# Attention of a fused layer: probabilities turned by DMA and VectorE in place of TensorE

## The reference

```
kv_c = kv @ W_kvc                                     # 256 keys x 128
q_c  = q @ W_dq ; q_nope, q_rope = q_c @ W_uq, q_c @ W_qr     # 16 heads
scores = (q_nope . k_nope + rope(q_rope) . rope(k_rope)) * scale
good = (k_ids <= seg_id) & (k_ids >= seg_id - 8)
attn = softmax(where(good, scores, NEG))
out  = (attn @ v).reshape(b, lq, H * HD) @ W_o
x = x + out
```

## Time and profile before

| | |
|---|---|
| runs | 3063.78, 3070.87, 3072.26 us; median 3070.87 |
| profiled execution | 3065.81 us, its span 3064.0 us |
| PE busy | 3032.5 us, 99% |
| PE weight load / DVE / ACT / POOL busy | 86% / 73% / 45% / 40% |
| attention loop | about 1040 to 2355 us of the span |
| TensorE's clock | full, except 3.4 us at half speed about 1015 us and again about 2424 us |

### The profile page before, as it was taken

How to read it: one execution, slowest core, us unless ns; L and a number is a source line. 1 busy time by engine, 2 the same in 40 slices (tenths; PEclk the granted TensorE clock), 3 DMA queues, 4 the chain that set the end, 5 groups by cost and what they waited for, 6 DMA issues and landing times.

```text
span 3064.0 us, 50062 instructions
## 1 busy us (share of the span) xinstructions
PE 3032.5 (99%) x18181; PEld 2636.4 (86%) x18181; DVE 2248.4 (73%) x5504; ACT 1379.9 (45%) x3399; POOL 1224.1 (40%) x1190
## 2 busy tenths in 40 slices
PE   9999999999999999999999999999999999999999
PEld 6777777899899799999999999999998788888887
DVE  7989999755677788888888888888887533333342
ACT  4655555433566455555555555555555211111111
POOL 9999999454333433333222333333311111111120
PEclk9999999999999999999999999999999999999999
DMA  4444442298899511111111111111102211111110
GB/s 153 131 144 138 129 130 86 86 307 299 220 265 284 189 49 49 49 49 43 49 42 49 49 49 36 49 38 47 49 29 81 88 56 55 55 49 43 46 42 14
DMA packets 179011, 292.41 MB, mean 95 GB/s; under 512 B 22616, under 2 KB 73952, under 8 KB 178768
## 3 DMA queue, kind: packets, MB, share of 16 engines
q1 hardware_dynamic: 145200, 193.24, 20.4%
q0 software_dynamic: 23344, 77.35, 7.9%
q10 hardware_dynamic: 10224, 18.62, 1.6%
HBM read 177.38 MB, written 111.76 MB: 94 GB/s over the span
## 4 chain that ended last, share of the span: by engine, by line
PE 92%; DVE 3%; DMA 2%; POOL 1%; ACT 1%; issue 1%; SPq 0%; POOLq 0%; DVEq 0%
PE f_Y L559 4%; PE t_U L1818 4%; PE f_Y L560 4%; PE f_Y L562 4%; PE t_U L1819 4%; PE t_U L1820 4%; PE g_O L2640 4%; PE g_PH L2628 4%; PE g_PH L2627 4%; PE g_PH L2626 4%; PE g_O L2642 4%; PE g_O L2641 4%; PE t_T L1794 3%; PE f_Y L554 2%; PE t_PO L1804 2%; PE t_PO L1805 2%
## 5 line engine op out<-in xcount | busy, mean ns | idle before, releaser
L1954 ACT ACTIVATE t_pr<-t_sm,t_nb 128x256 f32<-128x256 f32 x512 | 256.7, 502 | 418.5 <-DVE t_nb L2176 418.5
L2372 POOL TENSOR_TENSOR t_r<-t_r 128x256 f32<-128x256 f32 x128 | 95.8, 749 | 696.7 <-DVE t_r L2155 387.5
L2696 DVE CAST g_hh<-g_hf 128x512 fp32r<-128x512 f32 x128 | 67.8, 530 | 382.0 <-PE g_O L2642 380.2
L2667 ACT ACTIVATE g_hf<-g_PH,b1g 128x512 f32<-128x512 f32 x128 | 88.1, 688 | 528.3 <-PE g_PH L2628 457.0
L1360 POOL TENSOR_TENSOR c_kf<-c_vt,c_ct 128x512 f32<-128x512 f32 x256 | 284.5, 1129 | 5.9 <-ACT c_vt L775 3.2
L2186 DVE TENSOR_SCALAR t_pr<-t_pr,t_rw 128x256 f32<-128x256 f32 x512 | 256.7, 501 | 18.1
L559 PE MATMUL f_Y<-c_kh,c_th 128*128 128x512 f32 x540 | 250.8, 465 | 0.0
L562 PE MATMUL f_Y<-c_kl,c_th 128*128 128x512 f32 x540 | 213.7, 396 | 0.7 <-DVE c_kl L1072 0.7
L560 PE MATMUL f_Y<-c_kh,c_tl 128*128 128x512 f32 x540 | 213.4, 395 | 0.0
L2640 PE MATMUL g_O<-g_w,g_hh 128*128 128x512 f32 x512 | 200.1, 391 | 5.0 <-DVE g_hl L2698 5.0
L1818 PE MATMUL t_U<-t_voh,t_oth 128*128 128x512 f32 x512 | 202.0, 394 | 0.0
(11 more groups left out here) (375 smaller groups left out, 9974.9 us busy)
## 6 DMA issues: line engine op xcount, KB each, us to landing
xs<-c_zero SPq DMA_DIRECT2D x71, 256.0 KB, 4.6
f_xg<-xs SPq DMA_DIRECT2D x284, 64.0 KB
ys<-f_yt ACTq DMA_DIRECT2D x71, 256.0 KB, 5.1
f_xg<-xn SPq DMA_DIRECT2D x40, 256.0 KB, 4.9
c_xt<-x SPq DMA_DIRECT2D x32, 256.0 KB, 3.5
c_cr<-ctx SPq DMA_DIRECT2D x32, 256.0 KB, 4.0
c_ct<-ctxh SPq DMA_DIRECT2D x32, 256.0 KB, 4.9
c_t<-kt SPq DMA_DIRECT2D x32, 256.0 KB, 5.0
```

## The change

- The probabilities are turned without TensorE. ScalarE now also does `normalise(N)` (t_pr from t_sm with the inverse sum as scale, written in the order of the store), VectorE only the reciprocals (`inverses`). SyncE stores t_pr to DRAM (fp, 256 KB, runs of 512 bytes) and, when the store has landed, loads it back as t_pq (256 KB, runs of 2 KB). VectorE turns the 32x32 blocks (t_ptq), ScalarE rounds (t_pth), GpSimd makes t_ptl.
- The queries of a head now stand in another order, so t_xo is loaded and stored in four DMAs of 32 partitions each, and the store of x3 moves from GpSimd's queue to SyncE; the store of x2 for later sequences moves from SyncE to GpSimd.
- The loop is one step deeper: av(N-3) and vo(N-5) where av(N-2) and vo(N-4) stood. t_T is free and serves as second t_PO.
- Order on each engine: turn, rounding and low part come first in the step (on VectorE behind the maxima), the rest behind. GpSimd's mix is cut in four parts over steps 11 to 14.
- At the end `dense_first(0, 0)`, the first block of the dense part, stands ahead of the last two vo. Six dummy matmuls (`keep_busy`) at N = 2 are gone. In dense group 0 the rows are stored and loaded two blocks earlier in SyncE's list.

```
     def pturn(N):                                   # VectorE
-        w.wait_ge(*A["pth", N])
-        ve.tensor_tensor(m.ptl[:, N % 2, :, :], m.T[:, :].rearrange("p (k c) -> p k c", k=2), f32(m.pth[:, N % 2, :, :]),
-                         ALU.subtract).then_inc(*V("ptl", N))
+        w.wait_ge(*Q[f"pl{N % 2}"]["pl", N])
+        w.wait_ge(*P["av", N - 2])
+        ve.transpose(m.ptq[:, N % 2, :, :].rearrange("p k q -> p (k q)").rearrange("p (k c t) -> p c k t", k=4, c=4),
+                     m.pq[:, N % 2, :].rearrange("p (c k f) -> p c k f", c=4, k=4)).then_inc(*V("pt", N))
...
+    def probabilities(N):                           # SyncE, in every step
+        w.wait_ge(*A["nm", 2 * N + 1])
+        w.wait_ge(*V["pt", N - 4])
+        sp.dma_start(d["fp"][N % 4].rearrange("(i p f) -> p i f", i=4, f=128),
+                     m.pr[:, N % 2, :, :, :, :].rearrange("p i k t f -> p i (k t f)")).then_inc(*Q[f"ps{N % 2}"]("ps", N))
+        w.wait_ge(*Q[f"ps{N % 2}"]["ps", N])
+        w.wait_ge(*V["pt", N - 2])
+        sp.dma_start(m.pq[:, N % 2, :], d["fp"][N % 4].rearrange("(p l) -> p l", p=128)).then_inc(*Q[f"pl{N % 2}"]("pl", N))
...
+    def normalise(N):                               # ScalarE
+        w.wait_ge(*Q[f"ps{N % 2}"]["ps", N - 2])
+        for t in range(2):
+            x, k4 = 2 * N + t, (2 * N + t) % 4
+            w.wait_ge(*V["rc", x])
+            ac.activation(m.pr[:, N % 2, :, :, t, :], m.sm[:, k4, :].rearrange("p (i k f) -> p i k f", i=4, k=2), ACT.Copy,
+                          scale=m.rw[:, k4, 1:2]).then_inc(*A("nm", x))
...
+    def pturn(N):                                   # GpSimd
+        w.wait_ge(*A["pth", N])
+        gp.tensor_tensor(m.ptl[:, N % 2, :, :], m.ptq[:, N % 2, :, :], f32(m.pth[:, N % 2, :, :]), ALU.subtract).then_inc(*G("ptl", N))
...
-    def pturn(N):                                   # TensorE
-        w.wait_ge(*V["nm", 2 * N + 1])
-        w.wait_ge(*V["vw", 4])
-        w.wait_ge(*V["ptl", N - 1])
-        for kb in range(2):
-            for t in range(2):
-                i = pe.transpose(m.T[:, 256 * kb + 128 * t:256 * kb + 128 * t + 128], m.pr[:, N % 2, t, 128 * kb:128 * kb + 128], ident)
-        i.then_inc(*P("pt", N))
...
-        if 1 <= N <= TOTAL:
-            pturn(N - 1)
-        if 2 <= N <= TOTAL + 1:
-            av(N - 2)
+        if 3 <= N <= TOTAL + 2:
+            av(N - 3)
-        if N == 2:
-            keep_busy(pe, m.PU[0], ident, 6)
+        if N == TOTAL + 2:
+            dense_first(pe, w, K, 0, 0)
...
-        if g + 1 < GROUPS and 6 <= k < 10:
-            dense_rows_out(sp, w, K, 4 * (g + 1) + k - 6)
-        if g + 1 < GROUPS and 7 <= k < 11:
-            dense_rows_in(sp, w, K, 4 * (g + 1) + k - 7)
+        r = k + 2 if g == 0 else k
+        if g + 1 < GROUPS and 6 <= r < 10:
+            dense_rows_out(sp, w, K, 4 * (g + 1) + r - 6)
+        if g + 1 < GROUPS and 7 <= r < 11:
+            dense_rows_in(sp, w, K, 4 * (g + 1) + r - 7)
```

More of the change, by code:

```diff
@@ L1599, in residual, with store @@
             w.wait_ge(*P["qcp", b + 1])
-        w.wait_ge(*Q["tx2"]["x2", b])
-        sp.dma_start(m.xo[:, :, :], halves_of(d["x2"][b])).then_inc(*Q["txo"]("xo", b))
+        w.wait_ge(*Q[kept(b)]["x2", b])
+        for c in range(4):
+            sp.dma_start(m.xo[32 * c:32 * c + 32, :, :], turned_rows_of(d["x2"][b], c)).then_inc(*Q["txo"]("xo", b, c))
+    def store(b):
+        w.wait_ge(*V["add", 2 * b + 1])
+        for c in range(4):
+            sp.dma_start(turned_rows_of(d["x3"][b], c), m.xo[32 * c:32 * c + 32, :, :]).then_inc(*Q["to"]("out", b, c))
+    def probabilities(N):
[6 more added lines that the diff above has]
+        sp.dma_start(m.pq[:, N % 2, :], d["fp"][N % 4].rearrange("(p l) -> p l", p=128)).then_inc(*Q[f"pl{N % 2}"]("pl", N))
     w.wait_ge(*K.PE["o2", STEPS - 1])
@@ L1633, in sync_attention @@
     segment(1)
-    for N in range(TOTAL + 4):
+    for N in range(TOTAL + 7):
         b, h = divmod(N, NH)
-        if N >= 4 and (N - 4) % NH == (12 if N - 4 < NH else 8):
-            residual((N - 4) // NH)
+        if N >= 6 and (N - 6) % NH == NH - 1:
+            store((N - 6) // NH)
+        if 5 <= N < TOTAL and (N - 5) % NH == (12 if N - 5 < NH else 8):
+            residual((N - 5) // NH)
         if N < TOTAL and b + 2 < B:
@@ L1647, in sync_attention @@
             keep(1)
+        if N < TOTAL:
+            probabilities(N)
         if N == TOTAL - 8:
@@ L1852, in tensor_attention @@
     weights(7)
-    for N in range(TOTAL + 4):
+    for N in range(TOTAL + 5):
         b, h = divmod(N, NH)
@@ L2003, in scalar_attention @@
     weights(7)
-    for N in range(TOTAL + 4):
+    for N in range(TOTAL + 5):
         b, h = divmod(N, NH)
         q4, r = divmod(N, 4)
+        if 4 <= N <= TOTAL + 3:
+            av(N - 4)
+        if 1 <= N <= TOTAL:
+            normalise(N - 1)
         if N < TOTAL:
             exps(N)
+        if 2 <= N <= TOTAL + 1:
+            pturn(N - 2)
         if b + 1 < B:
@@ L2243, in vector_attention @@
     weights(7)
-    for N in range(TOTAL + 4):
+    for N in range(TOTAL + 6):
         b, h = divmod(N, NH)
@@ L2248, in vector_attention @@
             maxima(N)
+        if 2 <= N <= TOTAL + 1:
+            pturn(N - 2)
+        if N < TOTAL and N % 2 and (N + 1) // 2 < TOTAL // 2:
+            qabs((N + 1) // 2)
+        if 4 <= N <= TOTAL + 3:
+            av(N - 4)
+        if N < TOTAL:
             if r == 3 and 4 * (q4 + 2) < TOTAL:
@@ L2334, in gather, with mix @@
                                   in_offset=bass.IndirectOffsetOnAxis(ap=idx[:, 2 * b + t, k:k + 1], axis=0)).then_inc(*Q[f"tyg{y[2] + k}"]("yg", 2 * b + t, k))
-    def mix(b, t):
+    def mix(b, t, ks=(0, 1)):
         y = gather_rows(m, b, t)
         x = m.xt[:, t, :]
-        for k in range(2):
+        for k in ks:
             w.wait_ge(*Q[f"tyg{y[2] + k}"]["yg", 2 * b + t, k])
@@ L2405, in gpsimd_attention @@
         q4, r = divmod(N, 4)
+        if 2 <= N <= TOTAL + 1:
+            pturn(N - 2)
+        if b + 2 < B:
+            if h == 10:
+                gather(b + 2, 0)
+            if h == 11:
+                mix(b + 2, 0, (0,))
+            if h == 12:
+                mix(b + 2, 0, (1,))
+                gather(b + 2, 1)
+            if h == 13:
+                mix(b + 2, 1, (0,))
+            if h == 14:
+                mix(b + 2, 1, (1,))
+                keep(b + 2)
+        if b + 1 < B:
+            if h == (0 if b else 3):
+                power(b + 1, 0)
+            if h == (1 if b else 4):
+                power(b + 1, 1)
         if N < TOTAL:
@@ L2410, in gpsimd_attention @@
                 rotate(2 * (q4 + 1) + 1)
-        if N >= 4 and (N - 4) % NH == NH - 1:
-            store((N - 4) // NH)
-        if b + 1 < B:
-            if h == (0 if b else 3):
-                power(b + 1, 0)
-            if h == (1 if b else 4):
-                power(b + 1, 1)
-            if b and h in (7, 8):
-                turned(b + 1, h - 7)
-        if b + 2 < B:
-            if h == 10:
-                gather(b + 2, 0)
-            if h == 12:
-                mix(b + 2, 0)
-                gather(b + 2, 1)
-            if h == 14:
-                mix(b + 2, 1)
+        if b + 1 < B and b and h in (7, 8):
+            turned(b + 1, h - 7)
         if N == TOTAL - 7:
@@ L2648, in tensor_dense @@
         g, k = divmod(n, BLOCKS)
-        if n < DSTEPS:
-            first(g, k)
+        if 0 < n < DSTEPS:
+            dense_first(pe, w, K, g, k)
         if n >= 2:
```

138 lines of the change are left out of this document (68 added, 70 removed).

## The result

The changed kernel takes 3155.82 us in the median of three runs, against 3070.87 before, a ratio of 1.0286 with the interval 1.0259 to 1.0313. The profiled execution has a span of 3154.1 us, 90.1 more than before's 3064.0.

What follows compares the result with a forecast made beforehand. TensorE, busy without a gap, bounds the attention loop. From the profiled 3065.8 us, -110 transposes, -0.7 dummy matmuls, -6.8 dense rows, +3 ends and +12 waits gave 2963.3, stated as 2965 for the median; range 2944 to 2985, chance 0.66.

Steps and rivals of the forecast that it cites:

- the chain of a head: Attention loop: turn to turn two heads later, through DRAM, takes 8.2 us against 9.26, leaving 1.0 us margin.
- the same 12 us: Attention loop: PE waits from clustered DMA transfers, with GpSimd's lateness included, cost 12 us over 14 sequences.
- The bursts: Steps 10 to 14: six 512 KB transfers a sequence, 1.5 us each, cost PE about 0.9 us a sequence.
- the margin of 2.5 loops: Steps 10 to 14: 2.5 us of chain slack absorbs part of the 4.5 us transfer delay; a turn comes 2 late.
- The first rival: Loads of steps 10 to 14 set the pace; PE waits 2 to 4 us a sequence: 2985 to 3020; chance 0.19.
- GpSimd was a rival: Steps 11 to 15: GpSimd's full backlog uncovered, 2.6 us a sequence, 36 us in all: 3000; chance 0.05.
- The signature that I named: Attention loop: late GpSimd would show as av waiting for t_ptl.
- The slower rival: DRAM round trip exceeds 5.1 us; slower past 7.0, +400 us at 10.2; chance 0.07, time above 3075.
- the dense rows: Dense group 0: rows stored and loaded two blocks earlier remove PE's wait and half clock, -6.8 us.
- The transposes: Attention loop: taking four transposes a head off PE saves 0.43 us a head, 110 us over 256 heads.
- The bounds of the sum: Whole kernel: all costs at their low bound give 2946 us, at the high bound about 3010.
- The ends: Loop's start and last heads: one more step to fill and some PE idling together add 3 us.

Runs made afterwards that it cites:

- e1: Changed kernel with turn, rounding, low part, av and vo one step later and 8 DRAM places instead of 4: 3151.56 us, ratio 1.0271.
- e11: Changed kernel with GpSimd's gather and mixing spread as in e9 and the rotation first, turn still at N-2: 3126.82 us, ratio 1.0191.
- e9: Against e6, GpSimd's gather and mixing pushed apart over more steps, the norm's sums three steps later: 2986.8 us, ratio 0.9744.
- e10: e9 plus ScalarE's and GpSimd's conversion of dense weight pairs 1 and 2 placed later at the loop's end: 2982.31 us, ratio 0.9727.
- e2: Changed kernel with xa, context, x2 loads and x3 stores issued from ScalarE's queue instead: 3113.93 us, ratio 1.0160.
- e3: Changed kernel fetching only an eighth of the columns of xa and context for sequences 2 to 15: 3130.05 us, ratio 1.0206.
- e6: e1 with x3 store a step earlier, next rows' turn a step later, rotation before mixing, fourth dense weight pair before last x3 store: 3060.34 us, ratio 0.9986.
- e7: Kernel before with only the rows of dense group 0 sent and fetched two blocks earlier: 3057.14 us, ratio 0.9976.
- e4: Kernel before with one of four transposes a head from the second head on, three quarters of turned probabilities left out: 3002.45 us, ratio 0.9790.

## Why the prediction was wrong

**The step that failed is the chain of a head**, "8.2 us against 2 x 4.63 = 9.26 ... 1.0 us of margin in two steps". I said that this chain would hold TensorE's pace. In the runs it does not: VectorE stands waiting for t_pq ahead of 104 of 228 turns; one step more of depth takes that wait from 156 us to 1.5 (e1); and depth with its repairs is worth 140 us where GpSimd's lumps are out of the way (e11 to e9).

In the changed kernel's trace, averaged over heads 32 to 237, there are 6.7 us from the end of ScalarE's second copy to the start of the turn, where I had 5.1: 0.4 until the store is issued, 3.0 from store to load (I had 2.2; in the earlier trace rows it is 2.4, the second load begins at 2496.90), 3.3 from load to turn (I had 2.9). From a turn's start to the end of the copies two heads later it is 4.15, where I had 3.1. Their sum, 10.8, proves nothing by itself: it is the distance of two turns, so it is twice the mean step in any kernel of this form, and 9.5 in e10, with 10.15 and -0.62. At their shortest the two are 4.8 and 2.7, so the way through DRAM and the durations were right for a head in which nothing is in the way. Two things were left out.

First, steps are not even. The mean lengths of steps 0 to 15 of a sequence, from the starts of the scores (sequences 1 to 13):

```
before   5.5 3.7 7.1 4.5 5.5 3.7 5.8 5.4 5.5 6.5 5.3 4.3 5.5 3.7 5.3 4.3   mean 5.11
e10      5.1 4.1 6.7 3.9 5.3 3.4 5.0 5.0 5.5 6.1 4.9 3.9 5.1 3.4 5.0 3.9   mean 4.77
changed  6.3 3.5 6.7 4.1 5.1 3.5 5.4 6.9 5.1 7.0 4.9 3.9 5.1 6.7 7.8 4.9   mean 5.43
```

Before's row could have been read before the change was run. With TensorE as the bound (e10), two neighbouring steps are 8.4 us (13 and 14) to 11.6 (8 and 9). In the short pairs the chain has 0.2 us of margin against my own 8.2, not 1.0; a margin taken from a mean counts the surplus of the long steps. Shortness alone does not cost, though: steps 4 and 5 are as short (8.5 us in the changed kernel, 8.7 in e10) and lose nothing. Of the 10.6 us that a sequence is longer than in e10, 6.1 are in steps 13 and 14, 1.9 in step 7, 1.2 in step 0, 1.0 in step 15 and 0.9 in step 9. Steps 13 and 14 are the short pair that also has the late probabilities of steps 10 to 13 and GpSimd's lumps. How much of the loss is due to the uneven steps by themselves was not measured.

Second, I named what stands behind the turn on VectorE as "t_qal" alone. TensorE pays for a late turn at t_otl (22 us) as much as at t_qal (23), and GpSimd, which I had put into the same 12 us, is paid beside them with 42 us, for t_r and t_ptl. The two are not separate, since a late turn also makes the low part late. But a turn in time does not help t_r: in e1 the wait for it is 33 us, from 1100 to 2250 us alone, against 18.5.

**The bursts were priced as bandwidth.** The total share was forecast at 0.52 and is 0.48 to 0.54; e10 moves the same bytes in less time. A mean share does not show what one transfer meets. From store to load a head takes 2.3 us undisturbed, but 5.6 on average at step 10, behind xa and context, and 5.4 at step 13, behind the four loads of x2, where the store is also issued 1.5 us late. "1.5 us of all DMA engines" each was the right size, 3 us for two; "less the margin of 2.5 loops" was not, since hardly any margin was there. The order in the queue is a part of the delay: with a queue of their own (e2) the two places are 4.3 and 4.2. Instead of 12 us for the bursts, e3 gives 26 for one of them and e2 36 in the loop. The first rival had this mechanism, and its price, 2 to 4 us a sequence, is what they give (26 / 14 = 1.9, 36 / 14 = 2.6); but it stood alone there, and so made the kernel slower than I thought, not slower than before.

**GpSimd was a rival at 36 us and a chance of 0.05.** In the changed kernel spreading its lumps is worth 29 us (e11), near that price; with depth it is what TensorE waits for, and spreading is worth 74 us (e6 to e9). The signature that I named, av waiting for t_ptl, missed half of it, the wait of qturn for t_r. The Trainium skill, GPSIMD Engine Reference, section Engine selection, gives elementwise work to VectorE, GpSimd being about twice as slow with two inputs. The low part agrees, 1.29 us against 0.685 before, and it is what TensorE waits for in e6; e9 shows that the queue can carry it once gather and mixing don't stand in a row.

**The slower rival** named 7.0 us as the round trip from which the kernel is slower. Measured are 6.7, and the kernel is slower by 2.8%: the mechanism is that rival's in the main, the place from which it decides was again taken from the mean step. It forecast a long landing at a high share of DMA; of the 1.6 us over my 5.1, 1.2 are before the load is issued, in a few steps of a sequence. The Trainium skill, VectorE: DVE Perf Modes, section Rules for kernel authors, would have had the 128x128 turns on TensorE, and for the kernel as changed it was right; e9 and e10 show that with the turns off TensorE the kernel is 2.6 to 2.7% faster (0.2% of it are the dense rows, e7), if the rest of the loop is laid out for it.

**The other terms.** The transposes: -87 instead of -110 (e4; e10's period gives the same, 81.73 - 76.25 = 5.5 us in 16 heads, 0.34 a head). The gap of the earlier trace rows held more than them. The dense rows: -6.8 forecast, -6.9 in the changed kernel, -7.7 alone (e7); the half clock there begins at 2428.1 us, not about 2424, and is gone in e7. The bounds of the sum were added wrongly by a little, 2948 and 3014 instead of 2946 and about 3010, which changes nothing. The ends: +3 forecast, +25.5 measured, of which 18.7 are the tail and 6.8 the dense entry:

```profile
PE g_PH L2664 <- ACT g_hf L2710: 6.8, 1, 6.8
```

I counted TensorE's cover of the last head. I did not look at the dense layer's weights, whose fetches now stand behind the last probabilities on SyncE, nor at the x3 store moved onto SyncE ahead of the fourth pair. ScalarE waits for the weights with the last heads' work behind it:

```profile
ACT g_w L2503 <- DMA g_stg<-f1w: 29.2, 8, 11.4
```

e10's edit of just this order took 8 us from the tail in the profiled executions. The half clock is the last: I had it only as a term of 1.8 us in the dense layer.

So the 90 us are the sum of about -87 for the transposes, -7 for the dense rows, +25 at the ends, and therefore some 160 us of new waits and lost clock in the loop. That last figure is a difference; seen directly, against e10's period, are 10.6 us a sequence, 159 us in 15. The record of waits comes to the same. From 1100 to 2330 us PE waits 113 us in 115 gaps, and the half clock costs 17. A gap is counted from a matmul's modelled end, 0.28 us after its start, where the next could start after 0.12, so each hides 0.16, 18 us together. That makes 148 us, against 10.6 x 14.2 = 150 for the sequences in that stretch.

**What stays open.** e6's four edits were run together with the depth. One of them, the turn of the next rows a step later, acts in step 7, where the changed kernel loses 1.9 us a sequence; it wasn't tried alone, so up to 27 us (14 x 1.9) of e6's 95 may be its own and not the depth's. Of the 140 between e11 and e9 hardly any can be: there step 7 is 5.3 us without it and 5.0 with it. How the loss divides between uneven steps, transfers and GpSimd is not settled either, since their repairs don't add. The last 10 us of tail over before's 14.2 (24.6 in e10) weren't taken apart.

## What to carry to other kernels

Compare a chain with the shortest steps that it must fit over and with what else falls into them, not with the mean, and list all that is queued behind its waiting instruction on each engine: every entry is a place where the wait can come out. When a wait is taken away and the time stays, look for the next wait at the same steps before dropping the theory; here depth alone gave 4 us, spreading alone 29, and both, with the buffers freed that depth held too long, 169. A time that lies between two markers and is the same in every kernel by construction, as twice the mean step here, is no evidence for a chain; a wait that goes away with an edit is. Look at what stands ahead of a short transfer on a latency path in its queue: in e2 a queue of its own took away 1.3 of the 3.3 us of delay at step 10.
